# A float32 perceiver block on one Trainium2 core: the up projection issues both token halves under one stationary block

## The chip, the cores and the metric

The kernel runs on one core of one Trainium2 chip. The metric is the device time of one execution in microseconds (us), lower is better. The names of the engines are those of the profile: PE is the matrix engine and PEld its weight loads, DVE the vector engine, ACT the scalar engine, POOL the general-purpose engine, SP the engine whose queue issues most of the DMAs. A queue is written with a q (ACTq, SPq).

## The reference, cut to what matters

There are 16 x 64 = 1024 tokens of width 1024. Three residual steps follow each other: a cross attention over 1601 context rows, a gated feed-forward step with a top-k cut, and a small mixture of eight low-rank experts. The change is in the second one:

```python
z = layernorm(x)
s = silu(z @ w_gate.T)                       # 1024 x 2752
s = s with the 1376 entries of least magnitude in each row set to 0
s = s * (z @ w_up.T)                         # the up projection
x = x + s @ w_down.T
```

Each float32 product is made of three passes of the matrix engine: an operand is split into a high part and a low rest (hi, lo), and hi x hi, hi x lo and lo x hi are summed in PSUM.

## The kernel before, in words

The function `fast` holds everything that is timed here. It has one program for each engine, and the engines meet through counting semaphores. An engine's program is worked off in order, so whatever stands behind a waiting instruction waits too. The stages are attention, gate, up, down with the mixture woven into its last third.

**Up.** w_up is cut into UF = 21 blocks of 128 rows, numbered f. The 1024 tokens are two halves g of 512 columns. The transposed, normalised tokens z_hi and z_lo lie in SBUF as the moving operand, the block u_hi[f % 2], u_lo[f % 2] is stationary. Item i = 2f + g is one half of one block: 8 slices k of the width times 3 passes, 24 matmuls, all summed in PSUM bank i % 4. After its last matmul PE raises u_done by one.

**Who follows u_done.** ACT takes the items in order: it waits for u_done >= i + 1, copies the bank to u_out (L1785) and raises u_copied. SP stores each u_out to the matrix u_t in HBM (L1039). PE reuses a bank once its item is copied. POOL waits for all of block f - 2 before it splits block f into u_hi and u_lo (L1216, L1218), since both share a buffer; PE waits for u_lo_done before block f. SP loads block f + 2 (u_raw, L1033) when it comes to f in its program, after the store of block f - 1.

**The search that runs beside it.** DVE looks for each token row's cut magnitude during gate and up. It takes token tiles in pairs p = 0 to 3, with rounds r: DVE counts tile 2p below a trial cut (L1391) while ACT counts tile 2p + 1 (`compare`, L1745); both counts together give the next cut (L1420), for which `compare` of the next round waits. After six such rounds comes a last one without ACT, then the selection (L1428 to L1464), which raises `kept`. The places of ACT's part are written out by hand in terms of the items i; the places where SP stores a finished tile (sk, L1054), loads the next one (sx, L1050) and loads new magnitudes (mag, L1045) are written out in terms of the blocks f. SP waits there for `kept`, and its loads of u_raw stand behind that:

```python
UP_ABS_AT = {6: 4, 12: 5, 19: 6, 25: 7}                    # item i -> ACT takes magnitudes of tile t
UP_COUNT_AT = {0: (1, 0), 1: (1, 1), 2: (1, 2), 3: (1, 3), 4: (1, 4), 5: (1, 5),
               13: (2, 0), ..., 26: (3, 0), ..., 31: (3, 5)}  # item i -> compare(p, r)
UP_SK_AT = {1: 1, 5: 2, 7: 3, 12: 4, 13: 5, 18: 6}         # block f -> SP stores tile t, loads t + 1
UP_MAG_AT = {0: 4, 5: 5, 7: 6, 12: 7}
```

**The turn to down.** On ACT, the body for item i = 2 * UF - 2 = 40 is the one in which the first loads of the down stage are issued: two blocks of the cut s (t_sk, L1764) and four of u (t_u, L1778). The body for item 41 comes after them. In down, step n transposes a block of s (L2016), DVE multiplies it by t_u (L1494), ACT and DVE split the product (h_hi L1802, h_lo L1503), and PE makes 6 matmuls of 512 columns for each of three token tiles (L2032). There each stationary block h_hi or h_lo meets the two column halves of w_down, in two PSUM banks in turn:

```python
for a, (hp, wp) in enumerate(((h_hi, d_hi), (h_hi, d_lo), (h_lo, d_hi))):
    for o in range(2):
        last = pe.matmul(bank[2 * i + o][:, :], hp[jh][0:r, ts], wp[j][0:r, o * 512:(o + 1) * 512], ...)
```

Of the kernel before, what the change touches and what calls it, by code (L numbers as in the profile page):

```python
# [30 lines left out]
DK = D // P  # L31
# [15 lines left out]
UF = I // P  # L47
# [586 lines left out]
def fast(nc, x, ctx_nat, ctx_t, mask, x1, w_gate_up, w_up_t, w_down, s, sk, u_t, router_wt, router_b, a_t, b_t, all_bad, out, out_stored):  # L634
# [3 lines left out]
    with ExitStack() as ctx:  # L638
# [30 lines left out]
        bank = [psum[:, i, :] for i in range(8)]  # L669
# [139 lines left out]
        u_lo_done = sem("u_lo_done")  # L809
        u_done = sem("u_done")  # L810
        u_copied = sem("u_copied")
# [425 lines left out]
        def _(dve):  # L1237
# [67 lines left out]
            def add_mask(g, hp):  # L1305
                p = g % PER
                h = 2 * g + hp
                r = key_rows(p)
                dve.wait_ge(scores_ready, h + 1)
                if h >= SLOTS:  # L1310
                    dve.wait_ge(exp_done, h + 1 - SLOTS)
                c0, c1 = (c for _, c in parts(p))
                if p == LAST:
                    m = mask_t[0:r, c0].rearrange("p k s -> p (k s)").unsqueeze(1).broadcast_to([r, 4, 256])
                    into = masked[0:r, h % SLOTS, :].rearrange("p (n q) -> p n q", n=4)
                    of = scores[0:r, h % SLOTS].rearrange("p h (c q) -> p (h c) q", c=2)
                else:
                    m = mask_t[0:r, c0:c1 + 1].rearrange("p c k s -> p (c k s)").unsqueeze(1).broadcast_to([r, 2, 512])
                    into = masked[0:r, h % SLOTS, :].rearrange("p (h n) -> p h n", h=2)
                    of = scores[0:r, h % SLOTS]  # L1320
                dve.tensor_tensor(into, of, m, ALU.add).then_inc(mask_added, 1)  # L1321
# [525 lines left out]
        def _(pe):  # L1847
# [140 lines left out]
                    turn_z(q + 1)  # L1988
                gate(q)

            def up(i):
                f, g = divmod(i, 2)
                if i == 0:
                    pe.wait_ge(g_copied, SLOTS_G)
                if g == 0:
                    pe.wait_ge(u_lo_done, f + 1)
                if i >= 4:
                    pe.wait_ge(u_copied, i - 3)
                gs = slice(g * 512, (g + 1) * 512)
                for k in range(DK):  # L2000
                    for a, (wp, zp) in enumerate(((u_hi, z_hi), (u_hi, z_lo), (u_lo, z_hi))):
                        last = pe.matmul(bank[i % 4][:, :], wp[f % 2][:, k, :], zp[:, k, gs],  # L2002
                                         start=(k == 0 and a == 0), stop=(k == DK - 1 and a == 2))
                last.then_inc(u_done, 1)

            for i in range(2 * UF):
                up(i)

            def turn(n):
                gi, k = divmod(n, IC)  # L2010
# [887 lines left out]
```

## Time and profile before

| what | value |
|---|---|
| median of 3 runs | 1414.09 us (1413.16 to 1414.87) |
| the profiled execution, its own time | 1414.52 us |
| its span, first to last instruction | 1412.3 us |
| PE busy | 97% of the span |
| DVE, POOL, ACT busy | 69%, 67%, 52% |
| mean granted TensorE clock | 0.99 |
| up stage (matmuls of L2002) | from 852.3 us to 1087.7 us of the span |

Times of rows are in us from the start of the span. A timeline row gives the start, the length, the engine, the line, the operation, the tiles (out<-in), the shape and how many instructions are merged into the row; the bracket at its end is how long the engine was idle before it and who ended that. A waits row gives who waited for whom.

### The profile page before, as it was taken

The numbers are of one execution on the slowest core, as the hardware profiler recorded it, in microseconds if no ns is written. First come the engines' busy times: TensorE is split into PE (matmuls) and PEld (weight loads), VectorE is DVE, ScalarE is ACT, GpSimd is POOL, SyncE is SP. The second block draws the span as 40 slices with busy tenths as digits, with TensorE's granted clock in tenths as the row PEclk, the third lists the DMA queues.
The fourth block names the chain that finished last, engine by engine and source line by source line (L and its number), as shares of the span: only waits on it lengthen the run. The fifth ranks groups of instructions, "written<-read, shape, count | busy, mean of one in ns | idle before, by whom it ended". The sixth has DMA issues, their size and how long they took to land.

```text
span 1412.3 us, 30485 instructions
## 1 busy us (share of the span) xinstructions
PE 1367.9 (97%) x12727; PEld 1014.2 (72%) x12727; DVE 981.3 (69%) x1324; ACT 739.8 (52%) x935; POOL 942.9 (67%) x613
## 2 busy tenths in 40 slices
PE   4999999999999999899999999999999999999996
PEld 3555555555555555599999998888887888887874
DVE  6888888888888888870001898999997223255654
ACT  6788888888888888732224625243331111111211
POOL 0799888888888888813443342423334899999791
PEclk9899999999999999999999999999999999999998
DMA  9032423233323230024337348383837876865551
GB/s 357 28 103 104 137 98 112 101 115 104 117 100 121 98 107 17 16 77 166 141 123 299 122 163 289 112 286 114 279 120 245 300 256 190 270 191 181 154 192 53
DMA packets 110013, 217.58 MB, mean 154 GB/s; under 512 B 7200, under 2 KB 82864, under 8 KB 104880
## 3 DMA queue, kind: packets, MB, share of 16 engines
q1 hardware_dynamic: 88928, 192.89, 39.6%
q10 hardware_dynamic: 20944, 22.70, 5.2%
q8 instruction: 101, 1.65, 0.5%
q14 instruction: 40, 0.33, 0.1%
HBM read 173.63 MB, written 41.94 MB: 153 GB/s over the span
## 4 chain that ended last, share of the span: by engine, by line
PE 90%; DVE 3%; ACT 2%; DMA 1%; issue 1%; POOL 1%; SPq 0%; DVEq 0%; ACTq 0%; POOLq 0%
PE fast_psum L2002 17%; PE fast_psum L1895 16%; PE fast_psum L2032 15%; PE fast_psum L1913 15%; PE fast_psum L1980 15%; PE fast_psum L1932 6%; PE fast_psum L1939 1%; PE fast_psum L2062 1%; PE fast_psum L2016 1%; PE fast_psum L2083 1%; PE fast_psum L1918 1%; DMA fast_d_raw<-w_down 1%; ACT fast_below L1745 1%; PE fast_psum L1862 1%; ACT fast_g_hi L1717 1%
## 5 line engine op out<-in xcount | busy, mean ns | idle before, releaser
L1321 DVE TENSOR_TENSOR fast_masked<-fast_psum,fast_mask_t 128x1024 f32<-128x1024 f32 (+1 forms) x416 | 488.4, 1219 | 72.2 <-PE fast_psum L1895 70.6
L1177 POOL TENSOR_TENSOR fast_pair<-fast_probs 128x1024 f32<-128x1024 f32 x192 | 457.5, 2386 | 96.1 <-PE fast_psum L1932 47.6
L1658 ACT ACTIVATE fast_probs<-fast_masked 128x1024 f32<-128x1024 f32 (+1 forms) x416 | 438.0, 1058 | 68.6 <-DVE fast_masked L1321 53.6
L1895 PE MATMUL fast_psum<-fast_qT,fast_kraw 32*128 32x256 f32 (+1 forms) x3328 | 247.1, 403 | 6.8 <-ACT fast_qT L1605 3.2
L1913 PE MATMUL fast_psum<-fast_probs,fast_vraw 128*32 128x256 f32 (+1 forms) x3328 | 226.5, 386 | 0.8 <-ACT fast_probs L1658 0.8
L1895 PEld LDWEIGHTS fast_psum<-fast_qT,fast_kraw 32*128 32x128 f32 (+1 forms) x3328 | 153.7, 182 | 93.3 <-DVE fast_masked L1321 53.9
L1232 POOL TENSOR_TENSOR fast_d_lo<-fast_d_raw,fast_d_hi 128x256 fp32r<-128x256 f32 (+1 forms) x264 | 198.4, 781 | 5.3
L1208 POOL TENSOR_TENSOR fast_g_lo<-fast_g_raw,fast_g_hi 128x2816 fp32r<-128x2816 f32 x14 | 87.8, 6273 | 145.6 <-ACT fast_g_hi L1717 123.6
L1980 PE MATMUL fast_psum<-fast_g_hi,fast_z_hi 128*128 128x352 f32 x512 | 165.7, 324 | 1.7 <-POOL fast_g_lo L1208 1.7
L1980 PE MATMUL fast_psum<-fast_g_hi,fast_z_lo 128*128 128x352 f32 x512 | 165.7, 324 | 0.0
L1980 PE MATMUL fast_psum<-fast_g_lo,fast_z_hi 128*128 128x352 f32 x512 | 165.5, 323 | 0.0
L1913 PEld LDWEIGHTS fast_psum<-fast_probs,fast_vraw 128*32 128x32 f32 (+1 forms) x3328 | 87.1, 109 | 107.3 <-ACT fast_probs L1658 46.5
L1802 ACT CAST fast_h_hi<-fast_t_h 128x384 fp32r<-128x384 f32 (+1 forms) x66 | 31.6, 478 | 218.4 <-DVE fast_t_h L1494 206.2
L2002 PE MATMUL fast_psum<-fast_z_hi,fast_u_hi 128*128 128x512 f32 x336 | 133.0, 396 | 0.6 <-ACT fast_res L1708 0.6
L2002 PE MATMUL fast_psum<-fast_z_hi,fast_u_lo 128*128 128x512 f32 x336 | 132.9, 396 | 0.0
L2002 PE MATMUL fast_psum<-fast_z_lo,fast_u_hi 128*128 128x512 f32 x336 | 132.9, 395 | 0.0
L1494 DVE TENSOR_TENSOR fast_t_h<-fast_psum,fast_t_u 128x384 f32<-128x384 f32 (+1 forms) x63 | 32.2, 513 | 141.7 <-PE fast_psum L2016 135.9
L1216 POOL CAST fast_u_hi<-fast_u_raw 128x1024 fp32r<-128x1024 f32 x21 | 26.8, 1278 | 150.6 <-PE fast_psum L2002 109.0
L2032 PE MATMUL fast_psum<-fast_d_hi,fast_h_hi 128*128 128x512 f32 (+1 forms) x352 | 118.7, 419 | 1.1 <-issue 0.6
L1932 PE MATMUL fast_psum<-fast_pair,fast_ones 128*32 128x256 f32 x1536 | 118.1, 379 | 1.3 <-POOL fast_pair L1177 1.3
L2032 PE MATMUL fast_psum<-fast_d_lo,fast_h_hi 128*128 128x512 f32 (+1 forms) x352 | 110.0, 394 | 0.0
L2032 PE MATMUL fast_psum<-fast_d_hi,fast_h_lo 128*128 128x512 f32 (+1 forms) x352 | 109.9, 394 | 0.0
(164 smaller groups left out, 1903.3 us busy)
## 6 DMA issues: line engine op xcount, KB each, us to landing
fast_d_raw<-w_down SPq DMA_DIRECT2D x63, 512.0 KB, 4.0
fast_kraw<-ctx_t SPq DMA_DIRECT2D x32, 800.5 KB, 5.9
fast_vraw<-ctx_nat SPq DMA_DIRECT2D x16, 1536.0 KB
fast_g_raw<-w_gate_up SPq DMA_DIRECT2D x15, 1408.0 KB, 7.3
fast_mag<-s SPq DMA_DIRECT2D x8, 1376.0 KB, 9.8
fast_sx<-s SPq DMA_DIRECT2D x8, 1376.0 KB, 6.7
sk<-fast_sx SPq DMA_DIRECT2D x8, 1376.0 KB, 6.7
fast_u_raw<-w_up_t SPq DMA_DIRECT2D x21, 512.0 KB, 5.0
```

The source lines that it names most:

```text
L1177: pool.tensor_tensor(pair[:, n % PAIR_BUFS], both[:, :, 0, :], both[:, :, 1, :], ALU.add).then_inc(paired, 1)
L1208: pool.tensor_tensor(g_lo[j][:, :, :], g_raw[raw(n)][:, :, :], g_hi[j][:, :, :].bitcast(F32), ALU.subtract).then_inc(g_lo_done, 1)
L1232: last = pool.tensor_tensor(d_lo[j][0:r, qs], d_raw[j][0:r, qs], d_hi[j][0:r, qs].bitcast(F32), ALU.subtract)
L1321: dve.tensor_tensor(into, of, m, ALU.add).then_inc(mask_added, 1)
L1494: dve.tensor_tensor(t_h[n % 2][0:r, 0:w], bank[6 + n % 2][0:r, 0:w], t_u[n % TURNS][0:r, 0:w], ALU.mult).then_inc(h_ready, 1)
L1658: act.activation(probs[0:r, g % RING, hp * HALF:(hp + 1) * HALF], masked[0:r, h % SLOTS, :], ACT.Exp).then_inc(exp_done, 1)
L1895: last = pe.matmul(scores[0:r, (2 * g + hp) % SLOTS, h % 2, i * 256:(i + 1) * 256], kraw[b % BUFS][q, u, c * P:c * P + r], qT[q, b, u, :], ...
L1913: last = pe.matmul(o_acc[q, u, 0:256], vraw[b % BUFS][0:r, c, u * P + h * HD:u * P + (h + 1) * HD], probs[0:r, g % RING, (2 * h + i) * 256 ...
L1932: last = pe.matmul(o_acc[h * HD:(h + 1) * HD, u, 256:512], ones[:, :], pair[:, n % PAIR_BUFS, h, :], start=False, stop=final, skip_group_c ...
L1980: last = pe.matmul(bank[GATE_BANKS[q % GBANKS]][:, 0:GJ], zp[:, k, ts], wp[n % 2][:, k, :], start=(k == 0 and a == 0), stop=(k == DK - 1 a ...
L2002: last = pe.matmul(bank[i % 4][:, :], wp[f % 2][:, k, :], zp[:, k, gs], start=(k == 0 and a == 0), stop=(k == DK - 1 and a == 2))
L2032: last = pe.matmul(bank[2 * i + o][:, :], hp[jh][0:r, ts], wp[j][0:r, o * 512:(o + 1) * 512], start=(k == 0 and a == 0), stop=(k == IC - 1 ...
```

## The change

The up projection is issued block by block instead of item by item. Inside a block, each (k, pass) is issued for both token halves one after the other, so that two matmuls in a row have the same stationary block and write to two different banks. Both items of a block have their last matmul, and so their rise of u_done, at the end of the block. The waits stand at the head of the block: for u_lo_done as before, and from block 2 on for both copies of block f - 2. The number of matmuls and what they compute is the same, and the programs of the other engines are untouched.

```diff
-            def up(i):
-                f, g = divmod(i, 2)
-                if i == 0:
+            def up(f):
+                if f == 0:
                     pe.wait_ge(g_copied, SLOTS_G)
-                if g == 0:
-                    pe.wait_ge(u_lo_done, f + 1)
-                if i >= 4:
-                    pe.wait_ge(u_copied, i - 3)
-                gs = slice(g * 512, (g + 1) * 512)
+                pe.wait_ge(u_lo_done, f + 1)
+                if f >= 2:
+                    pe.wait_ge(u_copied, 2 * (f - 1))
                 for k in range(DK):
                     for a, (wp, zp) in enumerate(((u_hi, z_hi), (u_hi, z_lo), (u_lo, z_hi))):
-                        last = pe.matmul(bank[i % 4][:, :], wp[f % 2][:, k, :], zp[:, k, gs],
-                                         start=(k == 0 and a == 0), stop=(k == DK - 1 and a == 2))
-                last.then_inc(u_done, 1)
-
-            for i in range(2 * UF):
-                up(i)
+                        for g in range(2):
+                            last = pe.matmul(bank[(2 * f + g) % 4][:, :], wp[f % 2][:, k, :],
+                                             zp[:, k, g * 512:(g + 1) * 512],
+                                             start=(k == 0 and a == 0), stop=(k == DK - 1 and a == 2))
+                            if k == DK - 1 and a == 2:
+                                last.then_inc(u_done, 1)
+
+            for f in range(UF):
+                up(f)
```

## Rows read from the trace of the kernel before

**Rows 1.** The page's part 4, the chain that ended last: by engine, then by line.

```profile
PE 90%; DVE 3%; ACT 2%; DMA 1%; issue 1%; POOL 1%; SPq 0%; DVEq 0%; ACTq 0%; POOLq 0%
PE fast_psum L2002 17%; PE fast_psum L1895 16%; PE fast_psum L2032 15%; PE fast_psum L1913 15%; PE fast_psum L1980 15%; PE fast_psum L1932 6%; PE fast_psum L1939 1%; PE fast_psum L2062 1%; PE fast_psum L2016 1%; PE fast_psum L2083 1%; PE fast_psum L1918 1%; DMA fast_d_raw<-w_down 1%; ACT fast_below L1745 1%; PE fast_psum L1862 1%; ACT fast_g_hi L1717 1%
```

**Rows 2.** Busy time by windows, for L2002 alone: length, PE, PEld, clock, DMA share, GB/s.

```profile
864.00:1087.00 223.00, 223.00 (x957) 179.66 (x957) 1.00 0.58 194
```

**Rows 3.** Timeline of PE inside one down step, from its second pair to the next transposes.

```profile
1101.86 0.62 PE L2032 MATMUL fast_psum<-fast_d_lo,fast_h_hi 128*128 128x512 f32 x2
...
1105.53 0.49 PE L2016 MATMUL fast_psum<-fast_eye,fast_t_sk 128*128 128x128 f32 x3
```

**Rows 4.** Timeline of ACT and its queue at the last two items of up.

```profile
1082.17 0.59 ACT L1785 COPY fast_u_out<-fast_psum 128x512 f32<-128x512 f32 x1 [5.01 <-PE fast_psum L2002]
1082.18 0.94 ACTq L1764 DMA_DIRECT2D fast_t_sk<-sk  x2
1083.22 2.51 ACTq L1778 DMA_DIRECT2D fast_t_u<-u_t  x4
1087.78 0.59 ACT L1785 COPY fast_u_out<-fast_psum 128x512 f32<-128x512 f32 x1 [5.01 <-PE fast_psum L2002]
```

**Rows 5.** Timeline of all engines at the start of down.

```profile
1087.58 0.82 PE L2016 MATMUL fast_psum<-fast_eye,fast_t_sk 128*128 128x128 f32 x6
...
1089.10 1.07 DVE L1494 TENSOR_TENSOR fast_t_h<-fast_psum,fast_t_u 128x384 f32<-128x384 f32 x2 [5.38 <-DMA fast_t_u<-u_t]
...
1090.89 1.19 PE L2032 MATMUL fast_psum<-fast_d_hi,fast_h_hi 128*128 128x512 f32 x2 [0.57 <-issue]
...
1091.89 1.05 PE L2032 MATMUL fast_psum<-fast_d_lo,fast_h_hi 128*128 128x512 f32 x2
...
1092.74 1.05 PE L2032 MATMUL fast_psum<-fast_d_hi,fast_h_lo 128*128 128x512 f32 x2
...
1111.01 0.73 PE L2032 MATMUL fast_psum<-fast_d_hi,fast_h_hi 128*128 128x512 f32 x2 [0.54 <-POOL fast_d_lo L1232]
```

**Rows 6.** Windows at the start of down: length, the five engines' busy time, clock, DMA.

```profile
1090.00:1092.00 2.00, 1.43 (x6) 1.03 (x5) 1.73 (x4) 1.12 (x3) 0.00 (x0) 0.68 1.02 361
1092.00:1094.00 2.00, 2.00 (x6) 1.54 (x5) 0.02 (x1) 0.10 (x1) 0.11 (x1) 0.50 1.04 409
```

**Rows 7.** Timeline of DVE: the counts that begin rounds of the search.

```profile
863.00 3.08 DVE L1391 TENSOR_SCALAR_CACHE_REDUCE fast_below<-fast_mag,fast_cut 128x2752 bf16<-128x2752 f32 x1
...
868.77 3.08 DVE L1391 TENSOR_SCALAR_CACHE_REDUCE fast_below<-fast_mag,fast_cut 128x2752 bf16<-128x2752 f32 x1
...
891.18 3.08 DVE L1391 TENSOR_SCALAR_CACHE_REDUCE fast_below<-fast_mag,fast_cut 128x2752 bf16<-128x2752 f32 x1
...
950.73 3.08 DVE L1391 TENSOR_SCALAR_CACHE_REDUCE fast_below<-fast_mag,fast_cut 128x2752 bf16<-128x2752 f32 x1
...
955.62 3.08 DVE L1391 TENSOR_SCALAR_CACHE_REDUCE fast_below<-fast_mag,fast_cut 128x2752 bf16<-128x2752 f32 x1
```

**Rows 8.** Timeline of ACT: the copy of item 1 and the `compare` of round 1 behind it.

```profile
863.77 0.59 ACT L1785 COPY fast_u_out<-fast_psum 128x512 f32<-128x512 f32 x1 [2.12 <-PE fast_psum L2002]
864.26 2.59 ACT L1745 ACTIVATE fast_below<-fast_mag,fast_cut 128x2752 bf16<-128x2752 f32 x1
```

**Rows 9.** Timeline of SP's queue: a finished tile's store, the loads of blocks 8 and 16.

```profile
914.96 0.32 SPq L1054 DMA_DIRECT2D sk<-fast_sx  x1
...
922.24 0.60 SPq L1033 DMA_DIRECT2D fast_u_raw<-w_up_t  x1
...
1016.45 0.80 SPq L1033 DMA_DIRECT2D fast_u_raw<-w_up_t  x1
```

**Rows 10.** Timeline of POOL: the split of block 8, and where that of block 16 begins.

```profile
933.96 1.05 POOL L1216 CAST fast_u_hi<-fast_u_raw 128x1024 fp32r<-128x1024 f32 x1 [10.57 <-DMA fast_u_raw<-w_up_t]
935.08 2.41 POOL L1218 TENSOR_TENSOR fast_u_lo<-fast_u_raw,fast_u_hi 128x1024 fp32r<-128x1024 f32 x1
...
1024.91 1.05 POOL L1216 CAST fast_u_hi<-fast_u_raw 128x1024 fp32r<-128x1024 f32 x1 [11.90 <-DMA fast_u_raw<-w_up_t]
```

## The prediction, made before the changed kernel was run

> **What bounds the kernel now.** I read the page first. Nine tenths of the chain that ended last is PE, and its largest line is the one that the change rewrites, L2002 [rows 1]. So PE sets the end, and the question is how fast the up matmuls follow each other and what else keeps PE waiting. The windows answer the first: from 864 to 1087 us PE is busy without a gap at a granted clock of 1.00, which is the upper of its two levels, 2.4 GHz [rows 2]. From the end of item 1 (863.77 [rows 8]) to that of item 41 (1087.78 [rows 4]) are 40 items of 5.600 us, and 5.600 / 24 = 233.3 ns from one matmul to the next. Then I read the timeline at the end of up, because the change moves the moment at which ACT hears of item 40, and last the search, because it puts ACT's work into other places.
>
> **The interval of a matmul.** The change removes no matmul and no weight load: as many weight loads as matmuls stand there before [rows 2], and each matmul call still makes one. What changes is the order: two in a row share the stationary block, and the bank changes every time. Exactly this order stands in down, with the same shapes. From its second pair to the next transposes are 16 matmuls in 1105.53 - 1101.86 = 3.67 us, 229.4 ns each [rows 3]. That is 3.9 ns less than in up, and 3.9 ns x 1008 matmuls = 3.9 us. The trace does not say whether bank or operand placement makes the difference. The bounds are nothing, and the pure streaming time: at half the clock a pair takes 1092.74 - 1091.89 = 0.85 us, 425 ns each [rows 5], so 212.6 ns at full clock, 20.7 ns less than now, 20.9 us in all. I take 3.9 us, the row nearest in form.
>
> In down the sharing of the stationary block has plainly not brought the interval to 212.6. The Trainium skill (TensorE: Matmul & The Clock Gate, section "Step-by-step: what each phase is for") says that a stationary operand can be loaded once and used for many matmuls; by it up would come near the lower bound, by the down row it does not.
>
> **Blocks of w_up come later.** While DVE and ACT share a search, the rounds of pair 1 hang on ACT's copies. A round in which ACT is last takes 868.77 - 864.26 = 4.51 us from ACT's `compare` to DVE's next count [rows 7, 8]; one in which DVE is last takes 955.62 - 950.73 = 4.89 us [rows 7]. `compare` starts 0.49 us behind the copy in front of it [rows 8]. Now both items of a block are done together, item 2f some 0.23 us ahead of 2f + 1. Rounds 2 and 4 then wait for the ends of blocks 1 and 2, and 3 and 5 follow on: block 1 ends at 863.77 + 11.20 = 874.97, less 0.23 plus 0.49 is 875.2, + 4.51 = 879.7, + 4.89 = 884.6; block 2 ends at 886.17, so 886.4 + 4.51 = 890.9, + 4.89 = 895.8. The last round began at 891.18 [rows 7], so DVE slips by 4.65 us, or by 4.1 us when each block saves 48 x 3.9 ns = 0.19 us. The selection that follows waits for nobody but its own loads, so nothing makes the slip good, and I carry it on.
>
> What it delays: SP waits at block 5 for `kept` (it stored that tile at 914.96, right when DVE was done), and behind it stand the loads of sx and mag, two u_t stores and the load of block 8, issued at 922.24 [rows 9]. POOL was waiting for that block at 933.96 and had split it 3.53 us later [rows 10], 937.5. With 4.1 us it is 941.6; block 7 ends at 863.77 + 7 x 11.20 = 942.17, or 940.7 with eight blocks' savings, so PE waits 0.9 us. The same at block 16: load 1016.45 [rows 9], split from 1024.91 [rows 10] to 1028.4, now 1032.5; block 15 ends at 1031.77 before, 1029.7 with 3.0 us saved and 0.9 lost; PE waits 2.9 us. So 3.8 of the 3.9 us are given back, and up ends at 1087.7. Bounds: no wait at all (the slip is swallowed), or 3 us more than this, about one POOL or DVE instruction held up (the split of block 8 is 3.5 us long).
>
> **The end of up.** This part is surest. ACT's body for item 40 ran at 1082.17, one item ahead of PE's end; behind its copy, at once, were issued two loads of t_sk and from 1083.22 four of t_u, 2.51 us long [rows 4]. The first of t_u let DVE start at 1089.10 [rows 5], 6.93 us behind that copy. Item 40 now ends 0.23 us ahead of item 41. So DVE starts 6.93 - 0.23 = 6.7 us behind the end of up, where it was 1089.10 - 1087.78 = 1.32 us. From there to PE's first down matmul is unchanged, 1090.89 - 1089.10 = 1.79 us [rows 5]. **Cost: 5.4 us**, all on PE's path. PE's first transposes at 1087.58 [rows 5] must wait for t_sk too, but t_sk is issued ahead of t_u, so they hide in the same wait. The copy of item 41 comes behind the six issues, some 3.6 us later than before, and with it SP's store and loads; PE needs it only at its first down matmul, 8.5 us behind the end. Bounds: if the loads land faster, for there is less beside them, 3 us; if slower, 7 us.
>
> The clock: before, PE's gap was followed by half clock, 1.2 GHz, at 1092 [rows 6], and about 3.2 us of down matmuls at 425 ns cost 1.6 us. The gap now grows from 2.5 to 8 us. The loss may be the same, or up to twice that; I add 0.5 us (bounds 0 and 1.7). Against it, at 1111.01 PE waited 0.54 us for w_down's split [rows 5], behind loads that SP issues after its last u_t store; they slip by some 3.7 us, PE by 5.4, so that wait goes: -0.5 us.
>
> **The sum.** -3.9 (interval) + 3.8 (blocks 8 and 16) + 5.4 (end of up) + 0.5 (clock) - 0.5 (w_down) = +5.3 us. The profiled execution took 1414.52 us (span 1412.3), 0.4 us over the median of 1414.09. So 1419.8 on its own scale and **1419.4** on that of the median. Down itself, 5.4 us later, runs as before.
>
> **The rivals.**
> A, the forecast: as summed, 1419.4; chance 0.50, own range 1416.9 to 1422.5.
> B, no gain in the interval: what up and down differ in is not the order. Then the slip is 4.65 us, block 8 is just in time, block 16 is 1.3 us late: 1.3 + 5.4 = +6.7, 1420.8. For it: in up two of each three matmuls share their stationary block already (u_hi twice), and no gain shows there; chance 0.24.
> C, the gain stays: DVE's slip is made good on the way, so blocks 8 and 16 come in time: -3.9 + 5.4 = +1.5, 1415.6. For it: POOL then needs no more than what it has, 937.5 against 942.17. Chance 0.14; this is the case of no measurable change.
> D, other side: the shared stationary block removes the whole overhead, 20.9 us. With blocks 8 and 16 in time 1414.1 - 20.9 + 5.4 = 1398.6; with block 16 late as in A (ready near 1031, five blocks of 10.2 us behind it, up ends 1082, 5.8 us early) 1413.7. The kernel is faster by over 0.2% once up ends 8.2 us earlier, 8.1 ns a matmul, with blocks in time. Against it speaks 229.4 ns in down. Chance 0.05.
> E, the waits pile up: POOL and DVE hold each other up at blocks 8 or 16, or the first loads of down land at 7 us: 3 to 5 us over A, 1423.5. Chance 0.06.
> F, changing banks with every matmul lets PE pause and the clock fall. At half clock only a tenth of up, 100 matmuls, would cost 21 us, 1440. In down banks change in that way and the interval is 229.4 ns, which full clock alone allows. Chance 0.01. The Trainium skill (TensorE: Matmul & The Clock Gate, "A second HAM failure mode: psum-queue depth-cycling") tells of a 512-column kernel that cycled through banks, where the clock went back and forth; by that rule this change would lose, and this trace's down stage does not agree.
>
> **How the numbers follow.** 0.2%, 2.8 us, is about what a measurement tells from no change: the bounds are 1411.3 and 1416.9. Faster: most of D, 0.04. Same: C, the low end of A and the rest of D, 0.17. Slower: the rest, 0.79. The range leaves out D, F and the far ends of C and E: **1415.0 to 1423.5**.
>
> **What would show it.** In the changed profile: L2002 at 229 to 230 ns (B: 233, D: 213); all of ACT's copies in pairs; DVE's last round of pair 1 near 895.3; short waits of PE for u_lo at blocks 8 and 16 (C: none); t_sk and t_u issued behind the end of up and DVE waiting some 6.7 us for t_u; PE's first down matmul 8.5 us behind its last up matmul, against 3.1. The prediction is wrong if the loads at the turn land in half the time, or if the interval falls clearly below 229 ns with all blocks in time.

## The result, and the profile after

| what | before | after |
|---|---|---|
| median | 1413.75 us (1412.36 to 1415.02, 6 runs) | 1419.26 us (1416.94 to 1420.36, 6 runs) |
| ratio of times, 95% interval | | 1.0036 (1.0023 to 1.0048) |
| profiled execution, its span | 1414.52 us, 1412.3 us | 1417.13 us, 1415.5 us |

The change makes the kernel slower, by 5.5 us between the medians; by the ratio it is 5.1 us, with 3.3 to 6.8 us inside its interval. The forecast was 1419.4. The two profiled executions stand only 3.2 us apart in span, because that of before had a stretch of 3.4 us at half clock at 1302 us (1.7 us of loss) which the other had not; I therefore compare stage by stage. Executions of one kernel differ much like their mean granted clock: of the 31 of the kernel before that stand beside experiments 1 to 4, the fastest took 1411.17 us at 0.993 and the slowest 1421.19 us at 0.986, so 1 or 2 us between two small sets say little. The up stage starts 0.43 us earlier in the trace of after (851.85 against 852.28), and this has to be taken off wherever two times are compared.

The chain that ended last is still PE's (page, part 4; compare [rows 1]). The windows for the up matmuls alone show PE without a gap at a clock of 1.00, as before [rows 2]. ACT's copies show how long a block is:

```profile
PE 91%; DVE 4%; ACT 2%; issue 1%; DMA 1%; POOL 0%; DVEq 0%; ACTq 0%
```

```profile
864.00:1087.00 223.00, 223.00 (x958) 179.58 (x956) 1.00 0.57 189
```

```profile
863.12 0.59 ACT L1785 COPY fast_u_out<-fast_psum 128x512 f32<-128x512 f32 x1 [8.84 <-PE fast_psum L2000]
...
1087.12 0.58 ACT L1785 COPY fast_u_out<-fast_psum 128x512 f32<-128x512 f32 x1 [10.12 <-PE fast_psum L2000]
1087.12 0.96 ACTq L1764 DMA_DIRECT2D fast_t_sk<-sk  x2
1088.18 2.14 ACTq L1778 DMA_DIRECT2D fast_t_u<-u_t  x4
1090.41 0.59 ACT L1785 COPY fast_u_out<-fast_psum 128x512 f32<-128x512 f32 x1 [2.71 <-issue]
```

Between the first and the last of the copies that open a block lie 20 blocks of 48 matmuls: (1087.12 - 863.12) / 960 = 233.3 ns, to the tenth what it was. From the first up matmul to the start of the last one it is 235.07 us in both traces. So the up stage neither gained nor lost anything.

The rest of that fence is the turn [rows 4]: the body of item 40 runs when up is over, the loads stand behind its copy, and the copy of item 41 behind the loads. Who waits for them is in the timelines of PE and of DVE (compare [rows 5]):

```profile
1086.68 0.63 PE L2000 MATMUL fast_psum<-fast_z_hi,fast_u_lo 128*128 128x512 f32 x2
1090.85 1.54 PE L2016 MATMUL fast_psum<-fast_eye,fast_t_sk 128*128 128x128 f32 x6 [3.54 <-DMA fast_t_sk<-sk]
1093.83 0.88 PE L2016 MATMUL fast_psum<-fast_eye,fast_t_sk 128*128 128x128 f32 x3 [1.44 <-DVE fast_t_h L1494]
1095.68 1.19 PE L2032 MATMUL fast_psum<-fast_d_hi,fast_h_hi 128*128 128x512 f32 x2 [0.98 <-issue]
```

```profile
1093.12 0.56 DVE L1494 TENSOR_TENSOR fast_t_h<-fast_psum,fast_t_u 128x384 f32<-128x384 f32 x1 [5.00 <-DMA fast_t_u<-u_t]
1094.56 0.56 DVE L1494 TENSOR_TENSOR fast_t_h<-fast_psum,fast_t_u 128x384 f32<-128x384 f32 x1 [0.87 <-DMA fast_t_u<-u_t]
```

The last up matmul starts at 1086.92, the second of the pair at 1086.68. The first down matmul is 8.76 us behind it; before it was 1090.89 - 1087.34 = 3.55 us (the last up matmul there starts 0.44 us ahead of the copy of item 41). Here lie 5.2 us. "The gap" below is always this: from the start of the last up matmul to the start of the first down matmul.

The windows give the clock behind that gap (columns as in [rows 6]):

```profile
1095.00:1097.00 2.00, 1.32 (x3) 1.16 (x4) 1.60 (x4) 1.02 (x2) 0.00 (x0) 0.50 1.08 412
1097.00:1099.00 2.00, 2.00 (x6) 1.52 (x6) 0.00 (x0) 0.00 (x0) 0.31 (x1) 0.50 1.06 444
1099.00:1101.00 2.00, 2.00 (x8) 1.57 (x7) 0.00 (x0) 0.00 (x0) 1.92 (x3) 0.65 0.98 406
1101.00:1103.00 2.00, 2.00 (x12) 1.66 (x11) 0.40 (x1) 0.00 (x0) 1.62 (x3) 1.00 1.03 402
```

PE stood from 1087.3 to 1090.85; the clock was at half from 1090.2 and came back at 1100.4. The down matmuls from 1095.68 to 1100.4 ran at half clock, 4.7 us of them, which costs 2.35 us; before it was 3.2 us and 1.6. The matmul of 1111.01 [rows 5], which waited for w_down's split, starts at 1115.69 and waits no more. From the last up matmul to this one it is 28.77 us against 23.67, 5.1 us more. That is nearly the whole of the result.

### The profile page after: what moved, and what is told of

It reads as the page before. It is cut to its first block, busy times and chain, and to the rows that moved or that the text cites. A ratio compares the mean times of both kernels' runs of the same rounds, so it can differ in the third digit from the quotient of the medians.

```text
span 1415.5 us, 30485 instructions
## 1 busy us (share of the span) xinstructions
PE 1368.0 (97%) x12727; PEld 1014.4 (72%) x12727; DVE 980.8 (69%) x1324; ACT 738.1 (52%) x935; POOL 938.3 (66%) x613
## 4 chain that ended last, share of the span: by engine, by line
PE 91%; DVE 4%; ACT 2%; issue 1%; DMA 1%; POOL 0%; DVEq 0%; ACTq 0%
PE fast_psum L2000 17%; PE fast_psum L1895 16%; PE fast_psum L2032 16%; PE fast_psum L1913 15%; PE fast_psum L1980 14%; PE fast_psum L1932 6%; PE fast_psum L1939 1%; PE fast_psum L2016 1%; PE fast_psum L2062 1%; PE fast_psum L2083 1%; PE fast_psum L1918 1%; PE fast_psum L1862 1%; ACT fast_below L1745 1%; ACT fast_g_hi L1717 1%; PE fast_psum L1961 1%
## 5 line engine op out<-in xcount | busy, mean ns | idle before, releaser
L1216 POOL CAST fast_u_hi<-fast_u_raw 128x1024 fp32r<-128x1024 f32 x21 | 22.6, 1078 | 152.2 <-PE fast_psum L2000 88.1
L2000 PE MATMUL fast_psum<-fast_z_hi,fast_u_hi 128*128 128x512 f32 x336 | 105.7, 396 | 0.6 <-ACT fast_res L1708 0.6
L2000 PE MATMUL fast_psum<-fast_z_hi,fast_u_lo 128*128 128x512 f32 x336 | 105.7, 395 | 0.0
L2000 PE MATMUL fast_psum<-fast_z_lo,fast_u_hi 128*128 128x512 f32 x336 | 105.6, 396 | 0.0
```

The source lines that it names most:

```text
L2000: last = pe.matmul(bank[(2 * f + g) % 4][:, :], wp[f % 2][:, k, :], zp[:, k, g * 512:(g + 1) * 512], start=(k == 0 and a == 0), stop=(k == ...
```

## The experiments

Each run below comes with runs of the kernel before on the same chip. The medians of that kernel lie between 1413.75 and 1415.86 from one set of runs to the next, so only ratios to the runs beside it are compared. T is the theory that the whole loss comes from the place of the loads at the turn, the theories against it stand in the expectations.

**1. The changed kernel, its loads one body earlier.** ACT issues t_sk and t_u in the body of item 39, behind the end of block 19.

```diff
-                if i == 2 * UF - 2:
+                if i == 2 * UF - 3:
```

> The new order of matmuls, with ACT's six first loads of down (t_sk, t_u) moved from the body of item 40 to that of item 39, one block (11.2 us) ahead of the end of up. Theory T (the whole loss is the exposed loads at the turn, the order of the matmuls itself is worth nothing): the loss of 5.5 us goes, DVE waits for no load after up, PE's first down matmul comes 2.5 to 3.1 us behind the end of up, median 1412.5 to 1414.5. Rival R (the blocks of w_up, the search or the coupled copies lose time inside up): it stays slower, 1417 to 1419.

Measured: 1418.14 us (12 runs) against 1415.86 (31 runs), ratio 1.0015 (1.0001 to 1.0029). That is the ratio of experiment 3, which has the turn of the changed kernel in full, so the times do not show what this edit brings. The trace does: the gap is 5.69 us (1093.50 - 1087.81) instead of 8.76. Theory T had 2.5 to 3.1 us from the end of up and 1412.5 to 1414.5 us; neither came. PE's and POOL's timelines:

```profile
1088.04 0.82 PE L2016 MATMUL fast_psum<-fast_eye,fast_t_sk 128*128 128x128 f32 x6
...
1093.50 1.22 PE L2032 MATMUL fast_psum<-fast_d_hi,fast_h_hi 128*128 128x512 f32 x2 [2.50 <-POOL fast_d_lo L1232]
...
1089.24 1.04 POOL L1228 CAST fast_d_hi<-fast_d_raw 128x1024 fp32r<-128x1024 f32 x1 [19.77 <-DMA fast_d_raw<-w_down]
```

The transposes follow the end of up at once. Behind them appears a wait that the t_sk loads had covered: POOL got block 0 of w_down so late that it could cast it only at 1089.24. SP had issued its load at 1078.64, behind a store of sk that waits for the search; in the changed kernel it was issued at 1077.75, in the kernel before at 1073.39. So the turn has two inputs, and the change delays both: t_sk and t_u by the signal, w_down through the search. Not all of this wait is the search's, though: in the changed kernel POOL cast the block at 1085.71, 8.0 us behind the issue, here 10.6 us behind it. Here ACT issues the loads of t_u from 1078.08 to 1080.33, at the same time; that they slow w_down's is likely, but was not tried by itself.

**2. The old order, the loads one body later.** In the kernel before, the loads move from the body of item 40 into that of item 41, behind the end of up.

```diff
-                if i == 2 * UF - 2:
+                if i == 2 * UF - 1:
```

> The old order of matmuls and the old moments of u_done, with ACT's six first loads of down moved behind the copy of item 41, that is, to the end of up. Theory T: this alone makes the loss, PE's first down matmul 8 to 9 us behind the end of up (before: 3.1), median 1418.5 to 1420.5. Rival R: the late loads cost little on their own, 1414 to 1416.

Measured: 1422.24 us (8 runs), ratio 1.0040 (1.0025 to 1.0055). The loss of the change is there without its order of matmuls. It is even longer at the turn than theory T had it (8 to 9 us, and 1418.5 to 1420.5 us in all): first down matmul at 1102.16, a gap of 12.8 us. PE's waits (in total, times, longest):

```profile
PE fast_psum L2016 <- DMA fast_t_sk<-sk: 3.9, 1, 3.9
...
PE fast_psum L2016 <- DVE fast_t_h L1494: 3.2, 1, 3.2
...
PE fast_psum L2032 <- issue: 2.9, 1, 2.9
```

Here the loads of t_u are issued together with SP's last u_t store, its w_down load and its sk store, which the copy of item 41 lets go at the same moment. In the changed kernel that copy comes behind the loads, so SP's part is 3.3 us later. That this makes the difference between the two gaps is argued, not tried.

**3. The old order, both items announced together.** The matmuls stand as before. The first item of a block no longer raises u_done, the second raises it by two, and the wait for the copies is that of the change.

```diff
                 if i >= 4:
-                    pe.wait_ge(u_copied, i - 3)
+                    pe.wait_ge(u_copied, 2 * (f - 1))
...
-                last.then_inc(u_done, 1)
+                if g == 1:
+                    last.then_inc(u_done, 2)
```

> The old order of matmuls, but u_done rises by two at the end of each block and PE waits for both copies, as in the changed kernel. Theory T: the same time as the changed kernel, 1418.5 to 1420, since only the moment of the signal matters. Rival I (the order of matmuls or banks has an effect of its own, for or against): it differs from the changed kernel by more than 2 us.

Measured: 1418.63 us (12 runs), ratio 1.0015 (1.0003 to 1.0027). Its turn is that of the changed kernel, in PE's timeline:

```profile
1092.99 1.54 PE L2017 MATMUL fast_psum<-fast_eye,fast_t_sk 128*128 128x128 f32 x6 [4.52 <-DMA fast_t_sk<-sk]
...
1097.07 1.19 PE L2033 MATMUL fast_psum<-fast_d_hi,fast_h_hi 128*128 128x512 f32 x2 [0.22 <-issue]
```

8.99 us lie between the last up matmul (1088.08) and the first of down, against 8.76, and the interval in up is 233.3 ns. So the signals alone make the gap of the turn, and in the traces the order of the matmuls is worth nothing. By the ratio this kernel loses 2 us where the change loses 5; the intervals meet only at their edges, 1.0023 to 1.0027. The two medians themselves stand 0.6 us apart (1418.63 and 1419.26); the rest lies in the runs of the kernel before, 1413.75 us there and 1415.86 here. So the size of the loss is known no better than 2 to 5 us by the times, and what remains between the two stays open.

**4. Transposes ahead of the end.** In the kernel before, the loads move to the body of item 38, and PE makes the transposes of steps 0 and 1 before item 41; ACT takes its first h_hi before the copy of item 41.

```diff
-                if i == 2 * UF - 2:
+                if i == 2 * UF - 4:
...
-            for i in range(2 * UF):
+            for i in range(2 * UF - 1):
                 up(i)
...
             turn(1)
+            up(2 * UF - 1)
```

> The old order. The first loads of down are issued at item 38, PE makes the first two transposes of down before item 41 of up, and ACT makes the first h_hi before the copy of item 41. Theory T: PE's gap between up and down shrinks from 3.1 us to under 1.5 us and the clock does not fall there, worth up to 1.6 + 1.6 = 3.2 us; but w_down's blocks arrive as before, so that PE waits for the fifth one at about 1111 us and most of it is given back there: median 1412.5 to 1413.7. Rival W (w_down's blocks are no bound, for they shift too): 1410 to 1411.5.

Measured: 1416.61 us (12 runs) against 1415.86, ratio 1.0006 (0.9992 to 1.0019): no change, where theory T had a gain of a little over 1 us. The profiled execution is the fastest of the twelve, 1414.86 us. The gap at the turn has fallen to 1.16 us (1088.84 - 1087.68). But the time comes back in PE's timeline behind it, as waits for the split of w_down:

```profile
1100.09 0.98 PE L2035 MATMUL fast_psum<-fast_d_hi,fast_h_hi 128*128 128x512 f32 x2 [2.09 <-POOL fast_d_lo L1232]
...
1113.66 0.91 PE L2035 MATMUL fast_psum<-fast_d_hi,fast_h_hi 128*128 128x512 f32 x2 [2.82 <-POOL fast_d_lo L1232]
```

Each of them is followed by 3.4 us at half clock.

**5. The same, and the first load of x later.** SP's three loads of x for step 0 move to step 6, so that they do not stand beside the first blocks of w_down.

```diff
-        LOAD_X_AT = {0: 0, 12: 1, 30: 2}
+        LOAD_X_AT = {6: 0, 12: 1, 30: 2}
```

> The kernel with the first transposes of down ahead of item 41, and in addition the three loads of x (512 KB each) that stood between w_down's fourth and fifth block put behind the tenth. Theory W1 (in that kernel PE waited at about 1100 and 1114 us for w_down behind these loads, with half clock after each wait): the second wait goes, the first (behind the store of the last tile's s) stays, 1 to 3 us below it, so 1 to 2 us below the kernel before. Rival W2 (the store of s and the loads of u and s fill the DMA engines anyway): no more than 0.5 us.

Measured: 1414.63 us (11 runs) against 1414.93 (23 runs), ratio 0.9998 (0.9988 to 1.0009). The second wait is gone, the first, now at 1101.33, and its half clock remain. The forecast gain of 1 to 2 us did not show, and the interval reaches from 1.7 us faster to 1.3 us slower; on the time the run is inconclusive.

**6. The changed kernel with both inputs early.** Beside the edit of experiment 1, SP loads blocks 0 and 1 of w_down one block f earlier and ahead of the store of sk.

```diff
+                if f == UF - 3:
+                    for n in range(2):
+                        load_down(n)
                 if f in UP_SK_AT:
...
-                if f == UF - 2:
-                    for n in range(2):
-                        load_down(n)
...
-                if i == 2 * UF - 2:
+                if i == 2 * UF - 3:
```

> The new order, ACT's first loads of down one block early, and SP's loads of w_down's blocks 0 and 1 ahead of its wait for tile 6 of the search. Theory T2 (what was left of the loss with ACT's loads early is w_down's block 0, which stood in SP's queue behind the slipped search): POOL has split block 0 before the end of up, PE's first down matmul comes 2.5 to 3.5 us behind it, and the time is that of the kernel before within 1 us. Rival S (DVE itself is late through the slip, 1.5 to 2 us at the first multiplication): 1 to 2 us above the kernel before.

Measured: 1415.29 us (12 runs) against 1414.93, ratio 1.0003 (0.9991 to 1.0015). The loss is gone: with both inputs early the new order costs nothing, and brings nothing. The profiled execution is the slowest of the twelve (1419.94 us), so only its turn is read here. The first down matmul is 4.06 us behind the start of the transposes (1093.11 and 1089.05), where 2.5 to 3.5 us were expected; POOL had block 0 split by 1080. PE's waits:

```profile
PE fast_psum L2032 <- POOL fast_d_lo L1232: 2.6, 2, 2.1
...
PE fast_psum L2016 <- DVE fast_t_h L1494: 2.1, 1, 2.1
...
PE fast_psum L2000 <- POOL fast_u_lo L1218: 0.6, 1, 0.6
```

The 2.1 us for DVE are a third input of the turn: DVE was busy with the last tile of the search until 1091.31 and took t_h at once behind it, which is rival S of the expectation. The longer of the two waits for POOL stands at 1114.01 and is followed by 3.4 us at half clock.

**7 to 10. What the interval hangs on.** Four kernels with one timed execution each, on the step of the prediction that failed, the interval: 7 puts an unused tile of 64 bytes ahead of the large one, 8 lets the inner down steps use two banks instead of six, 9 and 10 exchange the changed kernel's moving and stationary operand in up. What 8, 9 and 10 compute is not the reference's result, and they serve for the interval alone.

```diff
+        sb("pad", [P, 16], F32)
         sb("slab", [P, SLAB], F32)
```

```diff
-                        last = pe.matmul(bank[2 * i + o][:, :], hp[jh][0:r, ts], ...
+                        b = 2 * i + o if k == 0 or k >= IC - 2 else o
+                        last = pe.matmul(bank[b][:, :], hp[jh][0:r, ts], ...
```

```diff
-                                             zp[:, k, g * 512:(g + 1) * 512],
+                                             g_lo[0].rearrange("p k j -> p (k j)")[:, 1536 + g * 512:2048 + g * 512],
```

```diff
-                            last = pe.matmul(bank[(2 * f + g) % 4][:, :], wp[f % 2][:, k, :],
+                            last = pe.matmul(bank[(2 * f + g) % 4][:, :], z_hi[:, k, f % 2 * P:(f % 2 + 1) * P],
```

> The kernel before with every large tile moved by 64 bytes in SBUF, no other edit. Before, the moving operand of up begins 64 bytes past a multiple of 128 and that of down at a multiple of 128; now it is the other way round. Theory P (placement makes the 3.9 ns between up's 233.3 and down's 229.4 ns): up falls to about 229.4 and down rises to about 233.3 ns. Rival: both stay.

> The kernel before, but in down all token tiles write to the banks 0 and 1 except in a group's first and last two steps, so the sums are not those of the reference; the count, shapes and order of matmuls stay. Theory B (down's interval is shorter because its banks change every six matmuls between pairs): from the second pair to the next transposes the interval rises from 229.4 to about 233.3 ns. Rival: it stays at 229.4 ns.

> The changed kernel, but the moving operand of every up matmul is 512 columns of a tile that lies in SBUF where down has one of its w_down blocks, in place of z_hi or z_lo. So the up projection is left out in value: its products are of other data, with the same count, shapes and order of matmuls. Theory P2 (the region of SBUF from which the moving operand is streamed makes the difference between 233.3 and 229 ns): up's interval falls to about 229 ns. Rival: it stays at 233.3 ns.

> The changed kernel, but the stationary operand of every up matmul is a 128-column slice of z_hi in place of the w_up block. So the up projection is left out in value, with the same count, shapes and order of matmuls. Theory P3 (the region from which the stationary operand is loaded, or that it is another tile than the moving one, makes the difference): up's interval moves away from 233.3 ns, to about 229. Rival: it stays at 233.3 ns, and what sets it stays open.

Measured: 7 and 8 leave 233.3 ns in up and 228.9 in down (1413.2 and 1412.67 us). 9 and 10 bring up to 227 ns (1416.65 and 1415.46 us). PE's timeline in down of 8, from the second pair of one token tile on over 14 matmuls, (1133.56 - 1130.36) / 14 = 228.6 ns with two banks:

```profile
1130.36 0.62 PE L2033 MATMUL fast_psum<-fast_d_hi,fast_h_lo 128*128 128x512 f32 x2
...
1133.56 0.49 PE L2016 MATMUL fast_psum<-fast_eye,fast_t_sk 128*128 128x128 f32 x3
```

PE's timeline in up of 9, (869.86 - 865.78) / 18 = 226.7 ns:

```profile
865.78 1.07 PE L2000 MATMUL fast_psum<-fast_g_lo,fast_u_hi 128*128 128x512 f32 x4
...
869.86 1.07 PE L2000 MATMUL fast_psum<-fast_g_lo,fast_u_hi 128*128 128x512 f32 x4
...
1092.12 1.54 PE L2016 MATMUL fast_psum<-fast_eye,fast_t_sk 128*128 128x128 f32 x6 [6.69 <-DMA fast_t_sk<-sk]
...
1095.86 0.77 PE L2032 MATMUL fast_psum<-fast_d_hi,fast_h_hi 128*128 128x512 f32 x1 [0.61 <-issue]
```

and of 10, (870.35 - 866.26) / 18 = 227.2 ns:

```profile
866.26 0.62 PE L2000 MATMUL fast_psum<-fast_z_lo,fast_z_hi 128*128 128x512 f32 x2
...
870.35 0.62 PE L2000 MATMUL fast_psum<-fast_z_lo,fast_z_hi 128*128 128x512 f32 x2
```

In 9, 10 and the changed kernel the order, the banks and the shapes are the same; only the operands differ. So it is the operands that decide, and whether the moving or the stationary one is exchanged makes no difference. What it is about them was not found: not a shift of all of them by 64 bytes (7). Besides the place in SBUF, 9 and 10 also change the data, and how often the operand changes: in 9 all passes and slices stream the same two pieces of g_lo, in 10 both operands are of z_hi in two passes of three. None of the three was tried apart, and each of these runs is a single one.

These two also show what a faster up would have been worth. PE waits for POOL's u_lo, 3.7 us in three waits in 9 (the row below, of its waits), 2.8 us in two in 10:

```profile
PE fast_psum L2000 <- POOL fast_u_lo L1218: 3.7, 3, 1.4
```

Of the some 6.6 us that the interval saves (6.6 ns x 1008), up keeps 2.1 us in 9 (852.04 to 1085.05) and 2.6 in 10. And the first down matmul comes at 1095.86 and 1095.32, hardly earlier than in the changed kernel (1095.68), since the wait for t_sk at the turn grows by 3.2 us: from 3.54 to 6.69 us in 9. There t_sk is issued at 1086.04 and PE goes on 6.1 us later, against 3.7 us (1087.12 and 1090.85); why the loads take longer was not tried.

**11. All inputs of the turn early.** Experiment 5, and beside it SP loads block 2 of w_down in the step of f = UF - 1, once POOL has split w_up's last block, and stores the last tile of sk at step 3 of down instead of at its head. POOL's wait for the end of up ahead of w_down's block 2 goes.

```diff
+                if f == UF - 1:
+                    sp.wait_ge(u_lo_done, UF)
+                    load_down(2)
                 store_up(f)
-            sp.wait_ge(u_done, 2 * UF)
-            load_down(2)
-            store_sk(TILES - 1)
             for n in range(STEPS):
+                if n == 3:
+                    store_sk(TILES - 1)
...
-                if n == DS - 1:
-                    pool.wait_ge(u_done, 2 * UF)
```

> The kernel with the first transposes of down ahead of item 41 and the loads of x late, and in addition w_down's block 2 loaded as soon as block 20 of w_up is split, its split no longer behind the end of up, and the store of the last tile's s behind w_down's fifth block. Theory W3 (the waits for w_down's blocks 2 to 4 and the half clock after them are what kept the earlier start of down from paying): PE goes from up into down with a gap under 1.5 us and without a wait or half clock up to 1130 us; 3 to 4.5 us below the kernel before, ratio 0.997 to 0.998. Rival: other waits take their place, 0.999 to 1.001.

Measured: **1409.86 us** (1407.8 to 1411.17, 6 runs) against 1415.43 (11 runs), ratio 0.9959 (0.9943 to 0.9975): faster than both kernels. PE's timeline at the turn, and the windows behind it:

```profile
1089.66 0.39 PE L2005 MATMUL fast_psum<-fast_z_hi,fast_u_lo 128*128 128x512 f32 x1
1089.89 0.49 PE L2019 MATMUL fast_psum<-fast_eye,fast_t_sk 128*128 128x128 f32 x3
1090.82 0.70 PE L2035 MATMUL fast_psum<-fast_d_hi,fast_h_hi 128*128 128x512 f32 x2 [0.44 <-ACT fast_u_out L1795]
```

```profile
1090.00:1110.00 20.00, 19.56 (x94) 15.97 (x93) 6.05 (x10) 3.64 (x7) 18.78 (x24) 1.00 0.95 351
1110.00:1130.00 20.00, 20.00 (x96) 16.42 (x95) 5.59 (x8) 2.08 (x5) 19.15 (x25) 1.00 0.85 301
```

The gap falls from 3.55 to 1.16 us (2.4), the half clock behind it goes (1.6), and so does the wait at 1111.01 (0.5): 4.5 us, inside the interval of the ratio (3.5 to 8.1 us). The medians stand 5.6 us apart, more than the 3 to 4.5 us expected. In the traces, from the last up matmul to the last of down, it is 293.1 us (1382.74 - 1089.66) against 300.1 (1387.42 - 1087.34); 1.7 of these 7.0 us are the half clock at 1302 us, which the trace of before has and this one has not, and 0.8 us stay open.

## Why the prediction was right, and where it was wrong

The time, 1419.4 forecast and 1419.26 measured, and the sign are right. But two terms of the sum were wrong and cancelled each other, -3.9 and +3.8, so that the forecast hit to 0.2 us is luck. The case that came is B, not A: no gain in the interval, and of B only the end of up.

- **The interval, -3.9 us: failed.** The step is "Exactly this order stands in down, with the same shapes ... I take 3.9 us, the row nearest in form". Measured are 233.3 ns and 0 us. The prediction said itself that the trace does not tell banks from operand placement; the experiments leave neither the order nor the banks. The old order and the new one both run at 233.3 ns (before and 3 against the changed kernel), down keeps its interval with other banks (8), and other operands alone bring up to 227 ns (9, 10). The row was nearest in form, but not in what decides. For B stood in the prediction that u_hi was shared already by two of three matmuls without a gain; that was the better evidence.
- **Blocks 8 and 16, +3.8 us: failed.** The search slipped by what was worked out: DVE's last round of pair 1 starts at 895.64 (forecast 895.3, and 895.8 for B), SP stores that tile at 919.43, 4.47 us later. But PE waits nowhere in up. Block 8 was split at 940.92, ahead of the 941.55 at which PE came to it, as B had it. For block 16 the step "nothing makes the slip good, and I carry it on" is wrong:

```profile
919.43 0.32 SPq L1054 DMA_DIRECT2D sk<-fast_sx  x1
926.31 0.61 SPq L1033 DMA_DIRECT2D fast_u_raw<-w_up_t  x1
...
1016.29 0.90 SPq L1033 DMA_DIRECT2D fast_u_raw<-w_up_t  x1
```

  Its load is issued at 1016.29, before at 1016.45 [rows 9]. The slip was lost in pair 2 of the search: its last round (the one without ACT) starts at 969.16, before at 968.64. With the 0.43 us of the earlier start of up added, a slip of 4.9 us has become one of 0.95. The trace of before shows where it had lost time that the other did not. Timelines of DVE, then POOL:

```profile
943.56 2.25 DVE L1420 TENSOR_TENSOR fast_cut<-fast_cut,fast_da 128x2 f32<-128x2 f32 x1
...
965.84 2.38 DVE L1416 TENSOR_TENSOR fast_db<-fast_off 128x2 f32<-128x2 f32 x1
...
968.64 3.08 DVE L1391 TENSOR_SCALAR_CACHE_REDUCE fast_below<-fast_mag,fast_cut 128x2752 bf16<-128x2752 f32 x1
...
943.39 2.40 POOL L1218 TENSOR_TENSOR fast_u_lo<-fast_u_raw,fast_u_hi 128x1024 fp32r<-128x1024 f32 x1
...
965.79 2.41 POOL L1218 TENSOR_TENSOR fast_u_lo<-fast_u_raw,fast_u_hi 128x1024 fp32r<-128x1024 f32 x1
```

  An instruction of two columns that lasts 0.16 us elsewhere lasts 2.25 and 2.38 us, from just behind the start to the end of POOL's L1218. The second hold-up is the one that counts. POOL's split starts when PE is done with a block, so DVE comes out of it at a moment that PE's blocks set. In all seven traces whose items are announced one by one (before, 2, 4, 5, 7, 8, 11) this hold-up is there, and the last round of pair 2 begins 116.4 to 117.0 us behind the first up matmul, although only two of them (before and 5) have the hold-up at 943.56 too. In the four that announce in pairs it begins at 117.3 (changed kernel), 117.8 (1), 118.6 (3) and 121.4 us (6). So what is left of the slip differs from run to run, from 0.9 to 5 us, and in 6, where it is longest, PE did wait 0.6 us for u_lo. A slip cannot be carried over ten blocks without looking where the old order itself has waits. The Trainium skill (SBUF — State Buffer, section "SBUF: two separate sides") states that a DVE operation with two SBUF inputs and a GpSimd operation that reads SBUF share a port pair by an exclusive lock: the one that starts first holds it for its whole instruction, and the other waits. These rows agree, 2.25 us beside POOL's 2.40 and 2.38 beside 2.41.
- **The end of up, +5.4 us: right, measured 5.2.** Its two parts were off by less than a us each. DVE starts 6.00 us behind the first copy of the pair (6.93 forecast), for the loads landed sooner; from there to the first down matmul it is 2.56 us instead of the 1.79 of before, for the second t_u came late too (0.87 us of DVE's wait). Experiments 2 and 3 show the mechanism without the new order; 6 takes the loss away from the new order, and 1 takes 3.1 us from its gap.
- **What the prediction did not have: w_down.** It worked out the slip of pair 1 and carried it on. But the rounds of pair 3 hang on the copies of items 26 to 31 in the same way, and make a new slip: the pair begins 0.4 us later than before (1010.97 and 1010.57), its last round 6.6 us later. DVE's timeline, before and after:

```profile
1041.65 3.08 DVE L1391 TENSOR_SCALAR_CACHE_REDUCE fast_below<-fast_mag,fast_cut 128x2752 bf16<-128x2752 f32 x1
```

```profile
1048.24 3.08 DVE L1391 TENSOR_SCALAR_CACHE_REDUCE fast_below<-fast_mag,fast_cut 128x2752 bf16<-128x2752 f32 x1
```

  SP's store of that pair's first tile waits for it (waits of SP's queue from 1050 to 1080 us, before and after), and behind the store stand the loads of w_down 0 and 1, 4.4 us later than before (1077.75 and 1073.39):

```profile
SPq L1054 <- DVE fast_sx L1464: 9.7, 1, 9.7
```

```profile
SPq L1054 <- DVE fast_sx L1464: 16.2, 1, 16.2
```

  In the changed kernel the wait for t_sk and t_u hides this; experiment 1 uncovers it, in a wait of 2.50 us that its own early loads may have made longer.
- **The clock, +0.5 us: right in kind, measured 0.75.** The half clock behind the gap costs 2.35 us against 1.6.
- **The wait at 1111.01, -0.5 us: right.** It is gone. It had put the matmul 1.02 us behind its transposes, now 0.25, so it was worth 0.77 us rather than 0.54.
- **The rest.** With 0 + 0 + 5.2 + 0.75 - 0.77 the traces give 5.2 us; from the last up matmul to step 4 of down 5.1 are seen, and the times give 5.1 by the ratio and 5.5 between the medians. Copies in pairs, loads behind the end of up and 8.5 us to the first down matmul (1095.68 - 1087.12 = 8.56 from the copy) came as said; the interval of 229 to 230 ns and the waits at blocks 8 and 16 did not.
- **The other rivals.** C and D fell with the interval, E did not come. F: the clock stays at 1.00 through all of up with banks that change at every matmul. The Trainium skill (TensorE: Matmul & The Clock Gate, section "A second HAM failure mode: psum-queue depth-cycling") tells of a clock that goes back and forth in a kernel that cycles through banks and whose PE idles briefly between groups of matmuls. Here PE does not idle in up, and the change of banks alone did not move the clock.

## What to carry to other kernels

When two pieces of work are interleaved, the signal of the first moves to the end of the second: look up everything that hangs on it, the loads at the next stage's head above all, and move those ahead before anything is gained by the new order. The turn between two stages is set by all its inputs together; here making t_sk early showed the late w_down, and only the version with all of them early was faster. Two matmul streams of the same shape and order are no measure for each other as long as their operands differ.

## What the runs showed of the hardware that was not expected

- Float32 products in three passes, 128x512 matmuls at full clock: 233.3 ns in up, 228.9 in down, 227 in up when one of the operands comes from another tile. Neither sharing the stationary block (233.3 both ways) nor the number of banks in use (228.9 both ways) changed the interval. What it is about the operands was not found.
- A DVE instruction on two columns took 0.16 us, or 2.25 and 2.38 us when POOL was in its L1218.
- The gap of 8.8 us at the turn was followed by 4.7 us of matmuls at half clock, the waits of 2.1 and 2.8 us in experiment 4 by 3.4 us each, and the gap of 1.16 us in experiment 11 by none. Between these the length alone does not decide: the gap of 3.55 us in the kernel before was followed by half clock, those of 2.93 us in experiment 7 and 3.31 us in experiment 8 were not, and neither was a wait of 2.25 us at 1111.35 in 7. So the half clock behind the old turn is not there in every execution.
